# Scores from keys and queries of 64 dimensions, two heads on half rows each, and the last two additions of the row sums on VectorE

## The reference

```python
h = layernorm(x)                                   # (4, 256, 128)
q = (h @ Wq), k = (ctx @ Wk), v = (ctx @ Wv)       # 8 heads of 64
attn = softmax(q . k * 64 ** -0.5) @ v             # per batch and head, 256 x 1601
x = x + attn @ Wo + bo
h = layernorm(x)
w = the two largest of softmax(h @ router_w + router_b), the others 0      # 8 experts
x = x + gelu(h @ sw1 + sb1) @ sw2 + sb2
      + sum over e of w[e] * (gelu(h @ rw1[e] + rb1[e]) @ rw2[e] + rb2[e])
```

## Time and profile before

| | us |
|---|---|
| median of 3 runs (lowest, highest) | 431.85 (431.66, 433.05) |
| the profiled execution, its own time | 430.69 |
| its span in the trace | 428.6 |
| busy: PE matmul | 421.8 (98%) |
| busy: PE weight load | 327.6 (76%) |
| busy: DVE | 279.9 (65%) |
| busy: POOL | 257.1 (60%) |
| busy: ACT | 218.2 (51%) |

### The profile page before, as it was taken

The page is one execution under the profiler, slowest core; times in us unless marked ns, Lnnn a source line. Parts: engine busy times, 40 slices in busy tenths (PEclk is TensorE's granted clock), DMA queues, the critical chain, the costliest instruction groups (busy, mean ns, idle before and its releaser), DMA issues.

```text
span 428.6 us, 7169 instructions
## 1 busy us (share of the span) xinstructions
PE 421.8 (98%) x2500; PEld 327.6 (76%) x2500; DVE 279.9 (65%) x556; ACT 218.2 (51%) x381; POOL 257.1 (60%) x174
## 2 busy tenths in 40 slices
PE   8999999999999999999999989999999999999997
PEld 7787777776887868777868777768777767778896
DVE  4786768786546859474348597754469597557653
ACT  3556253342663535335735242527624547689783
POOL 5518995878575749390756664463706460297981
PEclk9999999999999999999999998999999999999999
DMA  7400002000000020000000300000000011301500
GB/s 240 130 1 2 0 3 58 2 2 0 2 0 2 0 60 2 0 2 0 2 1 2 113 1 3 0 3 0 2 0 2 2 57 45 98 0 35 165 26 24
DMA packets 16329, 11.59 MB, mean 27 GB/s; under 512 B 9580, under 2 KB 13208, under 8 KB 16296
## 3 DMA queue, kind: packets, MB, share of 16 engines
q1 hardware_dynamic: 16296, 11.15, 9.5%
HBM read 10.55 MB, written 0.56 MB: 26 GB/s over the span
## 4 chain that ended last, share of the span: by engine, by line
PE 95%; DVE 2%; POOL 2%; ACT 1%; issue 1%; POOLq 0%
PE ps L1244 22%; PE ps L1164 12%; PE ps L1228 12%; PE ps L1229 11%; PE ps L1230 11%; PE ps L1076 8%; PE ps L1078 7%; PE ps L1077 7%; PE ps L1118 2%; PE ps L1176 1%; POOL g_lo L767 1%; PE ps L1084 1%; ACT ps L868 1%; DVE logit L1003 0%; PE ps L1094 0%
## 5 line engine op out<-in xcount | busy, mean ns | idle before, releaser
L842 ACT ACTIVATE probs<-ps 128x512 f32<-128x512 f32 (+1 forms) x208 | 123.8, 598 | 135.5 <-PE ps L1230 128.5
L969 DVE TENSOR_REDUCE maxes<-ps 128x1 f32<-128x402 f32 x256 | 131.8, 566 | 55.8 <-PE ps L1164 55.7
L562 POOL TENSOR_TENSOR work<-work,probs 128x1024 f32<-128x1024 f32 x54 | 128.9, 2387 | 19.5 <-ACT probs L842 16.8
L1244 PE MATMUL ps<-probs,v_sb 128*64 128x256 f32 (+1 forms) x832 | 93.4, 381 | 0.0
L560 POOL TENSOR_TENSOR work<-probs 128x1024 f32<-128x1024 f32 x14 | 33.5, 2390 | 86.2 <-issue 60.6
L1244 PEld LDWEIGHTS ps<-probs,v_sb 128*64 128x64 f32 (+1 forms) x832 | 58.4, 137 | 33.9 <-ACT probs L842 3.3
L1228 PE MATMUL ps<-g_hi,ctxT_hi 97*128 97x512 f32 (+1 forms) x208 | 83.4, 401 | 0.0
L1229 PE MATMUL ps<-g_lo,ctxT_hi 96*128 96x512 f32 (+1 forms) x208 | 82.5, 397 | 0.0
L1230 PE MATMUL ps<-g_hi,ctxT_lo 96*128 96x512 f32 (+1 forms) x208 | 82.1, 395 | 0.0
L1164 PE MATMUL ps<-ctxT_hi,g_hi 96*128 96x402 f32 x256 | 73.6, 359 | 2.0 <-DVE maxes L969 1.9
L1164 PEld LDWEIGHTS ps<-ctxT_hi,g_hi 96*128 96x128 f32 x256 | 46.9, 190 | 17.8 <-DVE maxes L969 5.1
(11 more groups left out here) (145 smaller groups left out, 524.6 us busy)
## 6 DMA issues: line engine op xcount, KB each, us to landing
v_sb<-weight_rows SPq DMA_DIRECT2D x12, 256.0 KB, 4.2
raw<-in_ctx_T_dram SPq DMA_DIRECT2D x3, 600.4 KB, 4.7
work<-in_L_ffn_rw_dram SPq DMA_DIRECT2D x1, 1024.0 KB, 7.0
raw<-weight_rows SPq DMA_DIRECT2D x4, 256.0 KB, 3.5
g_hi<-neg_row SPq DMA_DIRECT2D x60, 0.5 KB, 2.0
raw<-in_ctx_T_dram SPq DMA_DIRECT2D x3, 150.8 KB, 3.0
x_sb<-in_x_dram SPq DMA_DIRECT2D x1, 384.0 KB, 4.9
early<-in_WqkT_dram SPq DMA_DIRECT2D x1, 336.0 KB, 4.4
```

The lines of the kernel that those rows point to most:

```text
L562: ops.tensor_tensor(acc, acc, pr, ALU.add).then_inc(summed, 1)
L842: nc.scalar.activation(probs[0:rows, n % SLOTS, j, :], s_bank(chunk_no(*w))[0:rows, :], ACT.Exp, scale=SCALE).then_inc(probs_ready, 1)
L969: v.tensor_reduce(maxes[:, p % 2, i * T + t, blk:blk + 1], src[:, 0:BW], AX.X, ALU.max).then_inc(ring_taken, 1)
L1244: ins = mm(o_bank[DH * i:DH * (i + 1), :], v_sb[0:rows, c, h * DH:(h + 1) * DH], probs[0:rows, n % SLOTS, j, i * S:(i + 1) * S], start=(c ...
```

## The change

Keys and queries of 64 dimensions are formed for each pair: `q` is one ring item of three matmuls of 256 columns, `k` is four of three matmuls of 402 columns. For each of these five ScalarE makes the high part and VectorE the low part. The two heads of a pair lie on partitions 0 to 63 and 64 to 127. Scores of a unit are 4 products for each of its two chunks and each head, of 64 rows and 256 columns, issued for one head and the other by turns. The fourth product is of ones and the row of negated maxima. A unit fills two banks, one for each head, and there are two such pairs of banks. One exponential takes both banks. The maxima are matmuls of 64 rows, heads by turns. The ring has banks 4 to 6 in the attention.

The list is no longer made from durations but written out. For pair n: scores of unit u, two maxima of pair n+1 after each of the units 0 to 4, the quotients of pair n-1 after units 0 and 1; then `k` and `q` of pair n+2 (and v); other items; three maxima of pair n+2; all values; row sums; three more maxima of pair n+2. GpSimd adds units 1 to 4, VectorE the units 5 and 6, at the place of the values. In pair 0 GpSimd adds all, in the last pair VectorE. The products of weights are gone; Wq and Wk are loaded and split.

```diff
-WARM = 13
-REST_0 = 3
-REST_1 = 7
-REST_2 = 6
+WARM = 18
+REST_1 = 4
 TOP = 2
-RING = 4
-SCORE_BANKS = 3
+EARLY_MAXIMA = 3
...
+    maxima = [[("ring", ("max", b, p, i, t, k)) for k in range(blocks) for t in range(tiles)
+               for i in range(heads_per_pair)] for b, p in order]
+    couples = [maxima[0][i:i + heads_per_pair] for i in range(0, len(maxima[0]), heads_per_pair)]
+    def keys(n):
+        if n >= n_order:
+            return []
+        b, p = order[n]
+        return [("ring", ("k", b, p, 0)), ("ring", ("q", b, p))] + [("ring", ("k", b, p, k)) for k in range(1, blocks)]
+    first, second = keys(0), keys(1)
+    v0 = [("v0", c) for c in range(chunks)]
+    out = first[:2] + [("ctx0", 2)] + first[2:3] + [("ctx0", 3)] + couples[0] + couples[1] + first[3:4]
+    out += [("wv", 0)] + couples[2] + couples[3] + first[4:] + [("m", 0)]
+    for i, pair_of_maxima in enumerate(couples[4:]):
+        out += pair_of_maxima + v0[i:i + 1]
+    out.append(("shift", order[0]))
+    rest = v0[len(couples) - 4:]
+    out += rest[:2]
+    for i, x in enumerate(second):
+        out += [x] + rest[2 + i:3 + i]
+    out += rest[2 + len(second):] + maxima[1][:2 * EARLY_MAXIMA]
     for n, (b, p) in enumerate(order):
+        ahead = maxima[n + 1][2 * EARLY_MAXIMA:] if n + 1 < n_order else []
+        behind = 2 if n == 1 else 0
+        for u in range(n_units):
+            out.append(("scores", (b, p, u)))
+            out += ahead[:2]
+            if ahead and len(ahead) <= 2:
+                out.append(("shift", order[n + 1]))
+            ahead = ahead[2:]
+            if (n, u) == (1, 1):
+                out.append(("sums", order[0]))
+            if n and u in (behind, behind + 1):
+                out.append(("quotient", order[n - 1] + (u - behind,)))
+        vs = [("ring", ("v", b, c)) for c in range(chunks)] if p == 0 and b else []
+        projections = keys(n + 2)
+        if vs:
+            for i, x in enumerate(projections or vs[:1]):
+                out += ([x] if projections else []) + vs[2 * i:2 * i + 2]
+            out += vs[2 * len(projections or vs[:1]):]
+        else:
+            out += projections
+        if n == 0:
+            out += [("stats", t) for t in range(1, batches)]
         if n == 1:
+            out += [("normal", t) for t in range(1, batches)] + [("ring", ("xn", 0)), ("ring", ("xn", 1))]
+        if p == 1 and b + 1 < batches:
+            out += [("ctx", (b + 1, k)) for k in range(blocks)]
+        half, full = b * halves // batches - 1, b and b % (batches // halves) == 0
+        if b:
+            out += [("ring", ("y", b - 1))] * (p == 1) + [("ring", ("xt", b - 1))] * (p == 2)
+            if full and p == 3:
+                out += [("ring", ("router", half)), ("exp", half)]
+            if b - 1 and (b - 1) % (batches // halves) == 0:
+                out += [("rank", half)] * (p == 0) + [("ring", ("wrow", half))] * (p == 2)
+        if n == n_order - 2:
+            out += [("w2", e) for e in range(experts)]
+        out += [("w1", k) for k, at in enumerate((0, 2, 3)) if n == at]
+        following = maxima[n + 2] if n + 2 < n_order else []
+        out += following[:EARLY_MAXIMA]
+        out += [("values", (b, p, u, j)) for u, unit in enumerate(key_units(chunks)) for j in range(len(unit))]
+        if b and p == 1:
+            out += [("roots", b - 1), ("norm", b - 1)]
+        out += [("sums", (b, p))] * (0 < n < n_order - 1)
+        out += following[EARLY_MAXIMA:2 * EARLY_MAXIMA]
...
-    amid = range(kinds.index("scores"), len(kinds) - kinds[::-1].index("values"))
     ring_banks, ring_last, held = [], [], {}
     for n, (kind, w) in enumerate(steps):
         if kind == "ring":
             k = len(ring_banks)
-            wide = n in amid
-            late = n > kinds.index("first")
-            bank = min(range(O_BANK - (RING if wide else 2 if late else 3), O_BANK), key=lambda i: held.get(i, -1))
+            lowest = 2 if n < kinds.index("scores") else 4 if n < kinds.index("first") else 5
+            bank = min(range(lowest, O_BANK), key=lambda i: held.get(i, -1))
...
+        KQ = 2 * L + 4 * S
+        kq_hi, kq_lo = sb("kq_hi", [P, KQ], F32R), sb("kq_lo", [P, KQ], F32R)
+        (k_hi, q_hi), (k_lo, q_lo) = ((t[:, 0:2 * L].rearrange("p (a l) -> p a l", a=2),
+                                       t[:, 2 * L:KQ].rearrange("p (a s) -> p a s", a=4)) for t in (kq_hi, kq_lo))
...
+        ones_r = sb("ones_r", [P, P], F32R)
+        shift_rows = sb("shift_rows", [P, 2, S], F32R)
...
-        def s_bank(n):
-            return ps[:, n % SCORE_BANKS, :]
+        def score_banks(n):
+            return ps[:, 2 * (n % 2):2 * (n % 2) + 2, :]
...
-            if pair == 0:
-                return "pool"
-            return "dve" if u == NU - 1 or pair >= B * PAIRS - 2 or pair == B * PAIRS - 3 and u >= 4 else "pool"
+            return "dve" if pair and u >= NU - 2 or pair == B * PAIRS - 1 else "pool"
...
-                then_own(ops.tensor_tensor(acc[:, 0], acc[:, 0], acc[:, 1], ALU.add))
-                ops.tensor_tensor(acc[0:REST, 0], acc[0:REST, 0], pr[0:REST, 0], ALU.add).then_inc(summed, 1)
+                then_own(ops.tensor_tensor(acc[:, :, 0:S], acc[:, :, 0:S], acc[:, :, S:2 * S], ALU.add))
+                ops.tensor_tensor(acc[0:REST, :, 0:S], acc[0:REST, :, 0:S], pr[0:REST, :, 0:S], ALU.add
+                                  ).then_inc(summed, 1)
...
+                elif kind == "ring" and w[0] in ("k", "q"):
+                    act.wait_ge(ring_filled, ring_no[w] + 1)
+                    hi, _, src = key_parts(w)
+                    nc.scalar.copy(hi, src).then_inc(kq_hi_ready, 1)
...
-                    rows = P if UNITS[u][j] < FULL else REST
-                    nc.scalar.activation(probs[0:rows, n % SLOTS, j, :], s_bank(chunk_no(*w))[0:rows, :], ACT.Exp,
-                                         scale=SCALE).then_inc(probs_ready, 1)
+                    src, dst = score_banks(n), probs[:, n % SLOTS]
+                    if u == NU - 1:
+                        src, dst = src[0:REST, :, 0:S], dst[0:REST, :, 0:S]
+                    nc.scalar.activation(dst, src, ACT.Exp, scale=SCALE).then_inc(probs_ready, 1)
...
-                    add_probabilities(v, dve, then_own, (w[0], w[1], NU - 1, 0))
+                    add_probabilities(v, dve, then_own, (w[0], w[1], NU - 2))
+                    add_probabilities(v, dve, then_own, (w[0], w[1], NU - 1))
...
-                    elif w[0] == "g":
-                        hs = slice(2 * w[2], 2 * w[2] + 2)
-                        gv = src[0:C, :].rearrange("p (h s) -> p h s", h=2)
-                        hi = g_hi[0:C, b % 2, hs, :]
-                        v.tensor_copy(hi, gv).then_inc(g_hi_ready, 1)
-                        dve.wait_ge(g_hi_ready, b * PAIRS + w[2] + 1)
-                        v.tensor_tensor(g_lo[:, b % 2, hs, :], gv, hi.bitcast(F32), ALU.subtract
-                                        ).then_inc(ring_taken, 1)
+                    elif w[0] in ("k", "q"):
+                        dve.wait_ge(kq_hi_ready, hi_no[w] + 1)
+                        hi, lo, src = key_parts(w)
+                        v.tensor_tensor(lo, src, hi.bitcast(F32), ALU.subtract).then_inc(ring_taken, 1)
...
+                    elif w[0] == "q":
+                        cols, q = slice(w[2] * P, (w[2] + 1) * P), slice(b * S, (b + 1) * S)
+                        if w[2] == 0:
+                            pe.wait_ge(*(taken(("xn", 1)) if b else (setup_taken, 1)))
+                        ins = three(dst[:, 0:S], wq_hi[:, cols], wq_lo[:, cols], xnT_hi[:, q], xnT_lo[:, q])
+                    elif w[0] == "k":
+                        cols, first = slice(w[2] * P, (w[2] + 1) * P), min(w[3] * BW, L - BW)
+                        if (b, w[3]) == (0, 0):
+                            pe.wait_ge(*((w_rest_ready, 1) if w[2] else (w0_ready, 1)))
+                        pe.wait_ge(ctx_lo_ready, BLOCKS * b + w[3] + 1)
+                        ks = slice(first, first + BW)
+                        ins = three(dst[:, 0:BW], wk_hi[:, cols], wk_lo[:, cols], ctxT_hi[:, b % 2, ks],
+                                    ctxT_lo[:, b % 2, ks])
...
-                        ins = mm(dst[:, 0:BW], g_hi[0:C, b % 2, 2 * p + i, t * P:(t + 1) * P],
-                                 ctxT_hi[0:C, b % 2, k0:k0 + BW], start=True, stop=True)
...
+                        ins = mm(dst[:, 0:BW], q_hi[rows, pair % 4, t * P:(t + 1) * P],
+                                 k_hi[rows, pair % 2, k0:k0 + BW], start=True, stop=True)
...
-                    if n >= SCORE_BANKS:
-                        pe.wait_ge(probs_ready, n - SCORE_BANKS + 1)
-                    rows = P if c < FULL else REST
-                    ks = slice(c * P, c * P + rows)
-                    dst = s_bank(n)[0:rows, :]
-                    gh = g_hi[:, b % 2, 2 * p:2 * p + 2, :].rearrange("p h s -> p (h s)")
```

(24 more changed lines are left out.)

379 lines of the change are left out of this document (98 added, 281 removed).

## The result

The changed kernel takes 474.44 us (474.31 to 475.46, 4 runs), the kernel before 431.77 in the same comparison. The ratio is 1.0986 (95% interval 1.0960 to 1.1012): 9.9% slower. Forecast were 465 and slower, with 430 to 502 as the range. A few single executions here lay more than 1.5% above the fastest of their own kernel; medians hold them, ratios leave them out.

What follows compares the result with a forecast made beforehand. TensorE's work was taken to bound the kernel before, and its waits for other engines to lengthen the changed one. Profiled 430.7 + 27.3 (batches +24.6, start +2.7, end 0) + 6.8 for clock = 464.8, so 465 us; range 430 to 502.

Steps and rivals of the forecast that it cites:

- The direction and its cause: Whole kernel: slower, chance 0.81; a plain pair takes 21.65 us, 4.5 of it TensorE's waits, where it took 19.2.
- The two waits in the score stage: Plain pair's scores: TensorE waits for banks of maxima from 3.97 to 4.81 and 6.06 to 7.03 us.
- Two of the signs named beforehand: Attention: VectorE would be busy for 70% of it, TensorE well under 90%.
- Halves at once: Scores: two half-row matmuls of 256 columns run together in 0.12 us, so a unit takes 0.96, before 1.38.
- The quotients "do it": Score stage: two quotients amid VectorE's maxima make it end at 10.2 us; TensorE alone would end near 8.0.
- The start: Before the first scores: added casts, subtractions and maxima make scores begin near 27 us, not 24.3: +2.7.
- The end: Behind the attention: the experts keep their order, 0 us (-1 to +2).
- The clock: Attention: one fall to 1.2 GHz in every fourth pair, 4 x 1.7 = 6.8 us, bounds 0 and 54.
- The replay without clock: Four attention batches, step by step with banks and queues: +6.2, +8.05, +5.95, +4.4 = +24.6 us.
- The additions cost nothing: Beside the values: two additions moved to VectorE cost nothing if it reaches them 2.8 us before the row sums.
- TensorE's own sum, 17.1 against 18.9: One pair: TensorE's work alone, without waits for other engines, takes 17.1 us after the change and 18.9 before.
- the faster rival: Attention: the waits are covered after all, giving 395 us, or 427 with half of them; chance 0.16.

## Why the prediction was right

**The direction and its cause.** Right. The forecast had 21.65 us for a plain pair, 29.65 with v, 22.85 with `y` and 17.3 for the one without projections. At full clock the trace has 21.3, 29.7, 22.3 and 17.0. The two waits in the score stage (0.84 and 0.97 in the replay, of which the record of the matmul before covers some 0.2 to 0.3) are there as 0.56 and 0.75 in the plain pair shown, and the longer of them in almost every pair; the maxima in front of the values wait for the banks of the keys. Moving them out of that place gave back 20 us, about half of it clock, and halving VectorE's reductions 18, nearly all order. The chain of the forecast, quotient, maxima, bank, TensorE, was seen in VectorE's rows above. Two of the signs named beforehand were weaker than forecast: VectorE is busy for 67% of the attention and not 70, and TensorE for 91%, not "well under 90%".

**Halves at once.** Right in rate (0.12 for two, from the earlier trace rows). What I wrote of their starts, 0.01 apart and the next pair 0.12 later, was wrong: they are evenly 0.06 apart.

**The quotients "do it".** Only in part. The forecast named the two quotients amid the maxima as the cause of a stage of 10.2 and not 8.0. With them moved away the waits for the maxima went and came back in part as waits for low parts, net 1.2 us a pair of the 2.2 named and the 1.9 expected of the experiment. So their place is worth about half, and the rest is VectorE's sum of work, wherever it stands.

**The start.** Mis-sized. The term was +2.7 and measures +8.8. At 13.8 to 24.1 us the clock stood at 0.52, which costs about 5 us; the forecast had no clock in the start at all. That is half of the distance between 465 and 474. The other 3.7 us are 1.0 more than the term. The end, put at 0, took 2.2 more, of which 1.7 go with a fall of 3.4 us at 430.7.

**The clock.** This is the term that was mis-sized most. It was 6.8 us, four falls of 1.7 each. Over the attention the granted clock was 0.94, 0.93, 0.97 and 1.00 in the four batches. With 2 x (1 - clock) of each stretch at the lower level, that is 31 us at 1.2 GHz, at most 16 lost, nine times 1.7; with the start and the end it is some 20 by span times clock. The replay without clock, +24.6, may have been somewhat too large: 34.1 less 16 leaves at least 18 (20 if the 1.7 that the kernel before lost there is added back), and the undisturbed pairs are up to 0.55 us shorter than it had them (those with v 0.05 longer). That 465 comes within 2% of 474 thus owes something to luck: a replay that was if anything too long stands against a clock term less than half of what it should have been. Its ground, that falls follow the short waits of the ring, was not borne out: with these waits filled in part the clock stood at 0.97.

The page "TensorE: Matmul & The Clock Gate" of the Trainium skill says, in its section on psum-queue depth-cycling, that short idle times between groups of matmuls bring such falls. The start agrees: weight loads stood still ten times for 0.1 to 0.7 us between 8.2 and 13.6 us, matmuls for 0.45 at 9.9, and with work in these waits the clock held. In the attention filling them did not help, and what makes the clock fall there is left open. It held at 0.99 in the two kernels that either took the three maxima from before the values or gave unit 5 back to GpSimd, and in two of the three that did both, and not in those with later quotients (0.94), a shorter reduction (0.96) or a later normalization (0.97). Over whole executions it was 0.970 to 0.977 and 0.964 to 0.978 in the two and 0.953 to 0.957 in the changed kernel, but up to 0.982 with nothing but the start altered. I have one profile of each, and no common cause that fits all.

**The additions cost nothing.** Right for what I priced, the row sums, which waited for them once (1.4 us, at 396 us), and right in the kernel before (1.0015). Incomplete as a whole: I did not follow who else waits for the last addition. GpSimd's roots do, ScalarE's normalization waits for them, and the next pair's exponentials stand behind it. The price is small: 5.1 us of such waits, and 2.3 with unit 5 given back. The rest of that gain was clock.

**TensorE's own sum, 17.1 against 18.9.** Too low for any order tried, and this is why the faster rival did not come true even when mended: 19.3 us with TensorE standing still for only 0.4. A record covers the wait of the next matmul in part, so "busy" is not work at full rate. Seven maxima beside the scores instead of ten, and still two units of scores need 2.3 to 2.6 us where the sum has 1.9 and the maxima: with two pairs of banks the later units of a pair start when the exponential of the one before the last, 1.03 us long, is done. Three maxima between values cost 0.55 with the changes of tiling on either side; the expectation of 6.6 us for values and sums allowed 0.4 for all six. The 0.3 for changes of tiling in the sum came from no row.

## What to carry to other kernels

Fewer columns on the bounding engine are worth nothing until the order in which the helpers give back its buffers has been replayed: here a sum of TensorE's work said 9% less per pair, a replay of one pair with banks and queues said 13% more, and the trace gave 11% more. When a wait is removed by moving work on the engine that causes it, add up that engine's work up to the next common point; where the sum is the same, part of the wait comes back there (here 0.7 of 1.9 us). When the clock moves too, compare pairs that ran at full clock before you say what a change gained: the late quotients looked worthless and had shortened such pairs by 1.2 us, while unit 5's addition looked worth 10 us and had left them alone. And before an addition is called hidden, list everyone who waits for its result, not only the one on the shortest path.

## What the runs showed that I had not expected

- Four matmuls in a row on one half of the rows don't leave the other half idle: heads by turns and heads four by four gave the same rate, a start in 0.06 us, and 474.4 and 472.1 us. With the heads four by four, matmuls of the two halves started out of the order of the program.
- An exponential of 1024 columns over two banks took 1025 ns, one of 512 took 598: 0.43 us of 512 more columns, and a saving of 0.17 for each that is joined.
- VectorE's addition of 1024 columns took 1.22 to 1.25 us here and 1.36 in the earlier trace rows.
- A dozen small matmuls in the start's waits kept the clock at 1.00 up to the values of pair 0 in three profiles and gave 5 us; matmuls in the waits of the attention cost 15.
